# Five instruction lists of a small vision tower written out anew: front work of later tiles between the halves of gate/up, values in the logits' bank

## The reference

```
h   = patches(768) @ W.T + b                      # 16 x 64 x 256
v   = h @ w1.T + b1
w   = softmax((v @ ww.T + bw), over 31 taps)      # 16 heads x 31 taps
y   = causal convolution of v along the image axis, weights w per position and head
a   = layer_norm(h + y @ w2.T + b2) * gamma + beta
h2  = layer_norm(h + a)
g   = silu(bitlinear(h2, w_gate)) * bitlinear(h2, w_up)        # 1024 inner
out = layer_norm(h2 + bitlinear(g, w_down))
```

## Time and profile before

| | us |
|---|---|
| time, median of 3 runs | 152.15 (152.15 to 153.42) |
| the profiled execution's own time | 152.89 |
| its span | 151.0 |
| TensorE busy | 121.8 (81%) |
| VectorE, ScalarE, GpSimd busy | 98.0, 74.3, 53.7 |

### The profile page before, as it was taken

How to read it: one execution, slowest core, us unless ns; L and a number is a source line. 1 busy time by engine, 2 the same in 40 slices (tenths; PEclk the granted TensorE clock), 3 DMA queues, 4 the chain that set the end, 5 groups by cost and what they waited for, 6 DMA issues and landing times. The chain is left out here.

```text
span 151.0 us, 2274 instructions
## 1 busy us (share of the span) xinstructions
PE 121.8 (81%) x722; PEld 73.6 (49%) x730; DVE 98.0 (65%) x256; ACT 74.3 (49%) x113; POOL 53.7 (36%) x102
## 2 busy tenths in 40 slices
PE   7799999899989899898599599757966886667930
PEld 2385547655857736645363374345443362313520
DVE  5057769937407248849839655785688787897641
ACT  0311864682611139439827952883364454736410
POOL 7950002416614301701704440661651454404130
PEclk9999999999999999999999969978999999978995
DMA  4999992255323300121121113012210100100011
GB/s 133 397 333 434 419 412 92 47 57 209 35 51 57 32 4 0 35 26 15 35 25 10 35 45 29 7 36 50 20 32 0 39 0 0 35 0 17 25 35 35
DMA packets 22314, 12.44 MB, mean 82 GB/s; under 512 B 18013, under 2 KB 20317, under 8 KB 21918
## 3 DMA queue, kind: packets, MB, share of 16 engines
q1 hardware_dynamic: 21504, 10.72, 25.2%
q10 hardware_dynamic: 798, 1.58, 3.2%
HBM read 9.95 MB, written 2.34 MB: 81 GB/s over the span
## 5 line engine op out<-in xcount | busy, mean ns | idle before, releaser
L974 POOL TENSOR_SCALAR veps<-mv 128x1 f32<-128x1 f32 x24 | 5.8, 242 | 59.9 <-DVE mv L726 33.1
L610 ACT ACTIVATE silu<-bank,sc 128x512 f32<-128x512 f32 x16 | 11.0, 688 | 18.5 <-PE bank L417 18.5
L417 PE MATMUL bank<-w_q,q1T 128*128 128x512 bf16 x57 | 16.5, 412 | 3.2 <-ACT q1T L602 2.9
L439 PE MATMUL bank<-ident,gu 128*128 128x128 f32 x64 | 10.8, 298 | 7.6 <-ACT gu L574 7.5
L686 DVE TENSOR_REDUCE top<-bank 128x16 f32<-128x496 f32 x8 | 5.3, 667 | 17.5 <-PE bank L352 17.5
L298 PE MATMUL bank<-xT,tokW 128*128 128x256 f32 x72 | 16.3, 380 | 0.0
L366 PE MATMUL bank<-conv_w,vpad 128*32 128x128 f32 x256 | 15.7, 397 | 0.0
L298 PEld LDWEIGHTS bank<-xT,tokW 128*128 128x128 f32 x72 | 13.6, 190 | 2.6 <-issue 0.9
L352 PE MATMUL bank<-wl,h1T 128*128 128x496 f32 x32 | 14.6, 579 | 0.0
L581 ACT ACTIVATE q2T<-bank,minus_magic 128x512 bf16<-128x512 f32 x15 | 10.3, 689 | 7.5 <-PE bank L439 7.2
L975 POOL TENSOR_TENSOR rstd<-veps,minus_half 128x1 f32<-128x1 f32 x24 | 13.2, 549 | 2.0
(11 more groups left out here) (108 smaller groups left out, 231.2 us busy)
## 6 DMA issues: line engine op xcount, KB each, us to landing
xT<-in_xT SPq DMA_DIRECT2D x3, 768.0 KB, 14.7
w_raw<-in_wg SPq DMA_DIRECT2D x1, 1024.0 KB, 11.4
w_raw<-in_wu SPq DMA_DIRECT2D x1, 1024.0 KB, 13.4
w_raw<-in_wd SPq DMA_DIRECT2D x1, 1024.0 KB, 16.7
shear<-taps SPq DMA_DIRECT2D x8, 128.0 KB, 1.8
conv_w<-shear SPq DMA_DIRECT2D x64, 16.0 KB, 1.9
out_dram<-res SPq DMA_DIRECT2D x8, 128.0 KB
xT<-in_xT ACTq DMA_DIRECT2D x2, 384.0 KB, 5.6
```

The lines of the kernel that those rows point to most:

```text
L417: last = nc.tensor.matmul(out, q1T[:, t % 2, k, :], w_q[:, j, at:at + HALF], start=(k == 0), stop=(k == KC - 1))
L439: last = nc.tensor.transpose(ps_q2T(t, half)[:, k * P:(k + 1) * P], gu[:, t % 2, half, k * P:(k + 1) * P], ident[:])
L610: nc.scalar.activation(silu[:, t % 2, half, :], ps_gate, ACT.Silu, scale=sc[:, t % 2, 2:3]).then_inc(silu_ok, 1)
```

## The change

The loops go. Each engine's sequence is now one list of calls written out for the whole kernel, and each helper works out the waits that its place in the list needs (TensorE's `put` counts what is issued so far). What else changes:

- TensorE: `gate_up` is split in `gate(t, half)` and `up(t, half)`. Between the first two halves and the last two stand the residual and convolution of a later tile, or an inner transpose and `down`. The single halves of `inner_transposes` and `down` can stand apart. Tile 0's residual, logits, convolution and projection stand ahead of the embeddings of pairs 2 and 3. The eight late matmuls without use are gone.
- PSUM: values go to bank 2, the bank of the logits, instead of bank 1. The residual and projection have bank 1 alone. From tile 5 (LATE) the second half of the inner transposes uses bank 2; before it was tile 2.
- SBUF: `q2T` has two buffers, the scales `sc` four, the statistics and their inverse deviations two each.
- ScalarE: six function table loads instead of ten; halves of `silus` and `quant_inner` stand apart.
- SyncE: image part 1 is loaded ahead of the gate weights; the zero tails are written from `conv_w` behind GpSimd's memset instead of from `no_taps`; image part 3 is issued ahead of the first taps. `put_taps` is split from `spread`, and store 0 stands between `put_taps(7)` and `spread(7)`.

The diff, cut to its core (the helpers' new waits are shown where the prediction speaks of them):

```diff
-LEAD, SLOTS = 4, 4
-
-WARM_UP, WARM_LAST = 10, 8
+SLOTS = 4
+
+LAST = TILES - 1
+LATE = 5
...
-        q2T = sb("q2T", [P, KC_INNER, P], bf16)
+        q2T = sb("q2T", [P, 2, KC_INNER, P], bf16)
...
-        ps_down = bank[0][:, D:2 * D]
-        ps_v = bank[1][:, 0:D]
-        ps_attn = bank[1][:, D:2 * D]
+        ps_down = bank[0][:, 0:D]
+        ps_attn = bank[1][:, 0:D]
+        ps_v = bank[2][:, 0:D]
...
-            return bank[2 if half == 1 and t >= 2 else 5][:, :]
+            return bank[2 if half == 1 and t >= LATE else 5][:, :]
...
+            sp.dma_start(xT[:, 1], xT_d[1]).then_inc(x_in[1], 16)
             sp.dma_start(w_raw[:, 0], wg_d).then_inc(ffn_in[0], 16)
             sp.dma_start(w_raw[:, 1], wu_d).then_inc(ffn_in[1], 16)
-            sp.dma_start(xT[:, 1], xT_d[1]).then_inc(x_in[1], 16)
...
+            sp.dma_start(xT[:, 3], xT_d[3]).then_inc(x_in[3], 16)
+            put_taps(0); spread(0); put_taps(1); spread(1); put_taps(2); spread(2); put_taps(3); spread(3)
+            put_taps(4); spread(4); put_taps(5); spread(5); put_taps(6); spread(6); put_taps(7); store(0)
+            spread(7); store(1); store(2); store(3); store(4); store(5); store(6); store(7)
...
+                if put["logits"]:
+                    pe.wait_ge(shifted_ok, put["logits"])
...
+                if put["values"]:
+                    pe.wait_ge(v_ok, put["values"])
...
+            def gate(t, half):
+
+                if t == 0 and half == 0:
+                    pe.wait_ge(wq_gate_ok, 1)
+                pe.wait_ge(h1T_ok, put["embed4"])
+                pe.wait_ge(q1T_ok, t + 1)
+                if t > 0 or half > 0:
+                    pe.wait_ge(silu_ok, 2 * t + half)
+                for k in range(KC):
+                    at = k * INNER + half * HALF
+                    last = nc.tensor.matmul(ps_gate, q1T[:, t % 2, k, :], w_q[:, 0, at:at + HALF],
+                                            start=(k == 0), stop=(k == KC - 1))
+                last.then_inc(gate_ps, 1)
+                put["gate"] += 1
...
-            for i in range(-1, TILES + 2):
-                c, l, a, g = i + 1, i + LEAD, i, i - 2
-                if c < TILES:
-                    conv(c)
-                if i >= 0 and l < TILES:
-                    values(l)
-                if i == -1:
-                    embed(2, 0)
-                    embed(2, 1)
-                if i in (0, 1):
-                    embed(3, i)
-                if c < TILES:
-                    residual(c)
-                if 0 <= g < TILES:
-                    inner_transposes(g, 0)
-                if c < TILES:
-                    project_out(c)
-                if 0 <= g < TILES and g >= 2:
-                    inner_transposes(g, 1)
-                    down(g)
-                if 0 <= a < TILES:
-                    in_transposes(a)
-                if 0 <= g < 2:
-                    inner_transposes(g, 1)
-                if i >= 0 and l < TILES:
-                    logits(l)
-                if 0 <= g < 2:
-                    down(g)
-                if 0 <= a < TILES:
-                    gate_up(a)
-                if g == TILES - 2:
-                    pe.wait_ge(attn_read, TILES)
-                    keep_warm(bank[1][:, :], WARM_LAST)
...
+            embed(0, 0); embed(0, 1); logit_bias(); logit_weights(); values(0); residual(0); logits(0)
+            embed(1, 0); logits(1); weight_means(0, 2); embed(1, 1); values(1); embed(2, 0); logits(2); conv(0)
+            logits(3); project_out(0); embed(2, 1); weight_means(2, 3); residual(1); conv(1); values(2)
+            project_out(1); in_transposes(0); logits(4); gate(0, 0); up(0, 0); residual(2); up(0, 1); gate(0, 1)
+            logits(5); conv(2); values(3); project_out(2); in_transposes(1); embed(3, 0); gate(1, 0); up(1, 0)
+            residual(3); conv(3); up(1, 1); gate(1, 1); project_out(3); values(4); embed(3, 1); in_transposes(2)
+            inner_transposes(0, 0); logits(6); gate(2, 0); up(2, 0); residual(4); conv(4); logits(7)
+            inner_transposes(0, 1); project_out(4); up(2, 1); gate(2, 1); down(0, 0); down(0, 1)
+            in_transposes(3); inner_transposes(1, 0); values(5); gate(3, 0); up(3, 0); inner_transposes(1, 1)
+            residual(5); conv(5); down(1, 0); down(1, 1); project_out(5); up(3, 1); gate(3, 1); in_transposes(4)
+            values(6); gate(4, 0); up(4, 0); inner_transposes(2, 0); residual(6); conv(6); up(4, 1); gate(4, 1)
+            project_out(6); inner_transposes(2, 1); values(7); inner_transposes(3, 0); in_transposes(5)
+            down(2, 0); down(2, 1); inner_transposes(3, 1); gate(5, 0); up(5, 0); residual(7); conv(7); up(5, 1)
+            gate(5, 1); project_out(7); down(3, 0); down(3, 1); inner_transposes(4, 0); in_transposes(6)
+            gate(6, 0); up(6, 0); inner_transposes(4, 1); down(4, 0); down(4, 1); up(6, 1); gate(6, 1)
+            inner_transposes(5, 0); in_transposes(7); inner_transposes(5, 1); gate(7, 0); up(7, 0); up(7, 1)
+            gate(7, 1); down(5, 0); down(5, 1); inner_transposes(6, 0); inner_transposes(6, 1)
+            inner_transposes(7, 0); down(6, 0); down(6, 1); inner_transposes(7, 1); down(7, 0); down(7, 1)
...
+            out_h1T(0, 0); out_h1T(0, 1); out_wl(); out_v(0); weight_sum(0); weight_sum(1); exps(0)
+            out_h1T(1, 0); weight_round(1); exps(1); out_h1T(1, 1); out_v(1); weight_sum(2); weight_finish(1)
+            out_h1(0); exps(2); out_h1T(2, 0); out_yT(0); out_h1(1); exps(3); out_h1T(2, 1); out_yT(1); out_v(2)
+            out_q1T(0); nc.scalar.preload_act_table(ACT.Silu); silus(0, 0); out_h1(2)
+            nc.scalar.preload_act_table(ACT.Exp); exps(4); exps(5); out_yT(2)
+            nc.scalar.preload_act_table(ACT.Silu); silus(0, 1); out_v(3); out_q1T(1); out_h1(3); silus(1, 0)
+            out_yT(3); out_h1T(3, 0); silus(1, 1); quant_inner(0, 0); out_v(4); quant_inner(0, 1); out_h1T(3, 1)
+            out_q1T(2); quant_inner(1, 0); silus(2, 0); out_q2T(0, 0); out_h1(4)
+            nc.scalar.preload_act_table(ACT.Exp); exps(6); out_yT(4); quant_inner(1, 1); out_q2T(0, 1); exps(7)
+            nc.scalar.preload_act_table(ACT.Silu); silus(2, 1); out_q1T(3); out_q2T(1, 0); out_v(5); out_h1(5)
+            silus(3, 0); out_q2T(1, 1); out_yT(5); quant_inner(2, 0); silus(3, 1); out_q1T(4); out_v(6)
+            quant_inner(2, 1); out_q2T(2, 0); silus(4, 0); out_h1(6); out_yT(6); quant_inner(3, 0); silus(4, 1)
+            out_q2T(2, 1); quant_inner(3, 1); out_q2T(3, 0); out_q1T(5); out_v(7); out_h1(7); silus(5, 0)
+            out_yT(7); quant_inner(4, 0); out_q2T(3, 1); quant_inner(4, 1); silus(5, 1); out_q2T(4, 0)
+            out_q1T(6); silus(6, 0); out_q2T(4, 1); silus(6, 1); quant_inner(5, 0); quant_inner(5, 1)
+            out_q2T(5, 0); out_q1T(7); silus(7, 0); out_q2T(5, 1); silus(7, 1); quant_inner(6, 0)
+            quant_inner(6, 1); out_q2T(6, 0); out_q2T(6, 1); quant_inner(7, 1); out_q2T(7, 1)
...
+            bias_rows(LOGITS, BIASES); logit_bias_rows(); out_wl(); top_logits(0); shift(0); tap_sums(0)
+            tap_inverses(0); weight_scales(0, 2); top_logits(1); shift(1); weight_clip(1, wclip_up); tap_sums(1)
+            tap_inverses(1); weight_round(0); weight_clip(0, wclip_gate); top_logits(2); shift(2); tap_sums(2)
+            tap_inverses(2); top_logits(3); attn_stats(0); attn_variance(0); attn_centre(0); shift(3)
+            attn_norm(0); mid_stats(0); mid_variance(0); centre(0); mid_absmax(0); weight_scales(2, 3)
+            mid_scales(0); quant_in(0); tap_sums(3); tap_inverses(3); attn_stats(1); attn_variance(1)
+            weight_clip(2, wclip_down); attn_centre(1); top_logits(4); shift(4); attn_norm(1); mid_stats(1)
+            mid_variance(1); centre(1); mid_absmax(1); top_logits(5); shift(5); mid_scales(1); tap_sums(4)
+            tap_inverses(4); quant_in(1); inner(0, 0); attn_stats(2); attn_variance(2); inner(0, 1)
+            attn_centre(2); inner_absmax(0); attn_norm(2); inner_scales(0); mid_stats(2); mid_variance(2)
+            inner(1, 0); centre(2); mid_absmax(2); tap_sums(5); tap_inverses(5); attn_stats(3); mid_scales(2)
+            attn_variance(3); inner(1, 1); quant_in(2); attn_centre(3); inner_absmax(1); attn_norm(3)
+            inner_scales(1); mid_stats(3); mid_variance(3); top_logits(6); centre(3); mid_absmax(3); shift(6)
+            mid_scales(3); inner(2, 0); quant_in(3); tap_sums(6); tap_inverses(6); top_logits(7); shift(7)
+            attn_stats(4); attn_variance(4); attn_centre(4); tap_sums(7); tap_inverses(7); attn_norm(4)
+            inner(2, 1); mid_stats(4); mid_variance(4); down_result(0); out_stats(0); out_variance(0); centre(4)
+            mid_absmax(4); inner_absmax(2); mid_scales(4); inner_scales(2); inner(3, 0); quant_in(4)
+            attn_stats(5); down_result(1); out_stats(1); out_variance(1); attn_variance(5); inner(3, 1)
```

(74 more changed lines are left out.)

685 lines of the change are left out of this document (286 added, 399 removed).

## The result

The changed kernel takes 128.03 us (median of 4; 127.01 to 128.90) against 152.78 in the same runs: ratio 0.838 (0.830 to 0.846), 24.7 us less. The span of the profiled execution is 127.1 (its own time 128.9). The forecast was 133.5, with a range of 128 to 142. Ratios leave disturbed executions out (one of e8's seven, 151.5 us, is the grossest) and medians do not; where the two differ most (e3, e6, e13) the text goes by the ratio or by the undisturbed time.

A forecast was written before the change was run, and what follows sets the result against it. TensorE was taken as the bound, 32.7 us of its line lost, largely to each tile's chain. Work 112.6 + idle 9.8 + (a) 1.6 + (b) 0.7 + (c) 1.7 + tail 5.9 = 132.3; plus 1.15 offset: 133.5 us, range 128 to 142.

The forecast's parts named there:

- The walk: Hand timing of all five engines' new lists: TensorE's last matmul ends at 122.4 us; its case, 128 to 138, chance 0.66.
- one sign of being wrong: TensorE waiting for the DMA of conv_w, the taps of spread 7, was listed as showing the forecast wrong.
- the 112.6 us of TensorE's work: TensorE's whole work at full clock, summed from distances between starts of adjoining blocks in the earlier trace.
- (a): Readers start at a matmul's end, not one block distance after its start: ten steps on the end's chain, 1.6 us.
- (b): VectorE's quantization of q1 takes median 0.52, walked as 0.4: about six tiles behind 85 us, 0.7 us.
- (c): One half-clock spell on TensorE, after a gap like that before tile 5's transposes: 1.7 us, ends 0 to 5.1.
- Table loads: ScalarE's six loads instead of ten take 5.1 us less there, worth nothing by itself to the total.
- Values in the logits' bank: Values and logits wait for each other's bank 2 readers: 0.4 us uncovered, at logits 0; up to 10 if all uncovered.
- Store 0: On SyncE ahead of spread 7, whose taps land at 96.7 against convolution 7 at 98.2: cover 1.5 us.
- Rival 1: Strict lists stall each other, with VectorE back to back from about 85 to 119: 138 to 149 us, chance 0.22.
- Rival 2: Better than the walk: no half-clock spell and VectorE's late pieces covered, under 128 us, chance 0.06.
- Rival 3: The bank shared by values and logits becomes the bound: slower, over 153.7 us, chance 0.04.

The follow-up runs named there:

- e8: Changed kernel with eight matmuls without use in the gap ahead of tile 5's inner transposes: 127.60 us, ratio 0.831.
- e3: Changed kernel with both embeddings of the last pair moved to right behind embed(2, 1), their ScalarE evictions with them: 134.59 us, ratio 0.868.
- e6: Kernel before, with the last two gate/up halves of each tile but the last two behind the next pass's convolution: 165.5 us fastest, median 168.8, against 153.3.
- e13: Changed kernel plus the waits that values in bank 1 brought, values staying in bank 2: 135.75 us, ratio 0.880.
- e4: Changed kernel with spread(7) issued ahead of store(0): 128.04 us, ratio 0.834.
- e7: Changed kernel with ten table loads instead of six, the added ones ahead of exps(5) and exps(7): 131.12 us, ratio 0.853.
- e1: Changed kernel with each tile's four gate/up halves in a row, the work between them moved right behind: 132.85 us, ratio 0.866.
- e10: Changed kernel with another order behind 99 us, such as tile 7's q1 earlier and tile 4's statistics later on VectorE: 129.92 us, ratio 0.848.
- e5: Kernel before, loops kept, with inner transposes and down behind gate/up, ScalarE's order and buffers adapted, down's result read a pass later: 154.34 us, ratio 1.007.
- e2: Changed kernel with a single q2T buffer, evictions waiting for the down of the tile before: 129.83 us, ratio 0.846.
- e9: Changed kernel with e1, e2, e3 and e7 together: 141.80 us, ratio 0.923.

## Why the prediction was right, and where it failed

**The walk's mechanism held.** Milestones forecast and measured: first convolution 33.4 and 33.1; first gate 47.5 and 46.8; second gate/up done 62.4 and 61.4; last embedding done 67.1 and 65.9; convolutions 4 to 7 at 70.9, 81.6, 89.4, 98.2 and 69.7, 79.9, 87.6, 96.5; last gate 113.2 and 110.5; last matmul's end 122.4 and 121.2. The gaps forecast before gate 6 (1.1), the transposes of tile 5 (2.3), and tiles 6 and 7 (1.8) are 1.0, 2.0 and 1.9 in the trace. Those before down 4 (0.9) and before input transposes 7 and gate 7 (0.9) are only 0.2 and 0.3. The one spell at half clock behind 105 us came in the profiled execution. So did one sign of being wrong, a wait for the DMA of conv_w (0.6 before convolution 7), which e4 shows to cost nothing.

**The step that failed is two terms of the sum: the 112.6 us of TensorE's work, which measured 109.4, and the allowances (a) and (b), 2.3 us put on top, where the stretch that they were for lacked 0.3.** The sum was 132.3 of span and 127.1 was measured:

- *Block lengths.* Values were taken at 1.10 from 20.51 to 21.61, a pair with a short wait in it; where blocks adjoin it is 0.97 (77.34 to 78.31 above). Down was taken at 1.03, its length to the modelled end, where the distance to the next start is 0.87 (75.81 to 76.68). Gate/up was 1.77, with the change to the convolution in it, and is four times 0.43; embeddings 2.59, not 2.67. With eight of each (six embeddings) that is 1.0 + 1.3 + 0.4 + 0.5 = 3.2 of the 112.6: the work is 109.4. The walk carried the same long blocks, and is 1.7 late by convolution 7; it is 2.7 late by the last gate, the other 1.0 being mostly the two gaps that were smaller than forecast.
- *Allowances (a) and (b).* 2.3 us were put on top. At full clock (e8) the stretch from the last gate's first half to the last matmul takes 9.5; the walk alone had 9.2. Only 0.3 was missing there. Whether the walk had term (a), ten steps at 0.16, in its lengths already or something covered it, no run tells. For term (b), q1's quantization took 0.35 in the median of eight (0.27 to 1.46), not the 0.52 of the earlier trace rows.
- *Clock (c).* 1.7 taken, 1.3 measured (10.8 - 9.5).
- *Idle and tail.* With 109.4 of work and the last matmul ending at 121.2, 11.8 are idle or half clock; without the 1.3 it is 10.5, against 9.8. The tail is 5.9, as forecast.

By the walk: 2.7 late at the last gate + 2.0 of (a) and (b) + 0.4 of (c) = 5.1 of the 5.2. By the sum: 3.2 of work + 2.3 of (a) and (b) + 0.4 of (c) - 0.7 of idle time = 5.2. The range was too narrow at its low end for the same reason: 129.3 was called the case better than the walk, while all the allowances were on one side. The offset of times over spans (1.15 taken; median 128.0 over 127.1) left 0.2 more.

**Edits costed at nothing.** Two were wrong, though the walk contained them. Table loads were "worth nothing by itself": putting four back (e7) costs 3.1 by medians and 2.4 by ratios; in the trace q1T and a silu stand behind them, and TensorE waits 2.1 for that q1T. Values in the logits' bank were treated as a cost only, 0.4; what it takes away, the tie of values to VectorE's read of the projection and of the residual to the values' copy, is worth up to 6.4 to 7.7 in this order (e13). Store 0 was rightly nothing (e4), though not by its cover of 1.5: with convolution 7 due 1.7 earlier than walked the taps came 0.6 too late. The image part moved ahead and the tails were not tried alone; the first convolution is within 0.3 of the walk. The longest clip of a weight took 1.54 instead of 2.63; no wait of TensorE's hangs on it.

**The rivals.** Rival 1's picture, one late piece that makes others late in strict lists, is what e1, e3 and e10 show when the order is disturbed; in the order as written the gaps did not grow. Rival 2's time came by the ratio, but not for its reasons: the spell and most of the late gaps were there. Rival 3 (the shared bank as bound) did not come: logits waited 0.3 for the values' copy once. That the late inner transposes take away the 7.5 us of the earlier trace rows came true in the list of waits, but as the cause of a gain it does not stand alone: e5 gains nothing.

**What stays open.** e1, e2, e3, e7 and e13 sum to 20.7 (4.8 + 1.8 + 4.6 + 3.1 + 6.4) of 24.7, or all by ratios to 18.9, if e13 adds to the others as those four do (e9); that was not tried, and e13 is an upper bound. The rest, tile 0's early row with VectorE's new order among it, was not tried alone. Nor was the bank move with nothing else changed.

## What to carry over

Where several engines with strict lists pass a tile along, walk all the lists by hand with distances between starts of adjoining blocks, and add nothing on top that the trace does not show on that chain. Here the walk alone gave 128.3 with its tail, within 1% of the 127.1, but partly by luck: 3.2 us of too long blocks stood in for the spell (1.3) and the idle time (0.7) that it lacked. A wait's total beside one releaser is not a gain; taking it away in one list moved it to the next (e5), and the same split gained 4.8 in one order and cost 12 in another (e1, e6). A list of waits that counts from modelled ends also hides short ones: e1's 2.1 us before the second gate halves stand in it as 0.2. Look for a bank that ties two stages of different tiles together before looking at the stage with the longest wait.

## What the runs showed of the chip

A gap of 1.99 us before the transposes of tile 5 was followed 1.5 us later by a half-clock spell (0.50 in the window above); eight matmuls without use in it, 1.9 us, kept the clock at 1.00. In the tail reordered (e10) that gap is gone, and no spell stands there either. The kernel before had eight such late matmuls and three spells, this one none and one. The two ratios, 0.838 and 0.831, show that filling it is worth less than its cost in one profile, since by the estimate at e8 two of four executions had no spell.

Of table loads the changed kernel's ScalarE timeline (start, length, line) shows:

```profile
70.43 0.37 ACT L591 COPY h1b<-bank 128x256 f32<-128x256 f32 x1
70.82 1.28 ACT L640 ACT_TABLE_LOAD   x1
72.11 0.62 ACT L578 ACTIVATE probs<-probs 128x496 f32<-128x496 f32 x1
```

The copy ends at 70.80, the load starts 0.02 behind it and the exponential 0.01 behind the load. The Trainium skill (ScalarE: Activation LUTs, What ACT_TABLE_LOAD costs) has the same 1.28 for the load and a drain of about 1.38 beside it; here there is no room for one, so a switch takes 1.3 of ScalarE, and four of them 5.1.
